# A recurrent spiking block with a top-2 mixture: expert 0 and the bias rows move from VectorE's sums to ScalarE reads and accumulating DMAs

## What is computed

```python
# attention-like part
R, K, V = x @ Wr.T, x @ Wk.T, x @ Wv.T          # then spikes by lif_scan
h = 0.9 * h + k * v;  y = r * h                  # over the 512 steps
x1 = layernorm(x + y @ Wo.T, g1, b1)
ffn = lif_scan(lif_scan(x1 @ W1.T + b1) @ W2.T + b2)
x2 = layernorm(x1 + ffn, g2, b2)
x3 = _layernorm(x + x2)
# mixture of 8 experts, the 2 best per token
gates = top-2 of softmax(x3 @ Wg + bg), normalised
moe = sum over e of gate[e] * (x3 @ We[e] + be[e])
out = _layernorm(x3 + moe)
```

## Time and profile before

| | |
|---|---|
| median of 3 runs | 1124.46 us (1119.31 to 1125.79) |
| the profiled execution, its own time | 1122.8 us |
| its span, first to last instruction | 1120.9 us |
| busy: PE / PE weight load / DVE / ACT / POOL | 86% / 83% / 91% / 49% / 64% |
| mean granted TensorE clock | 0.946 of 2.4 GHz |
| accumulating DMAs on POOL's queue | 192 of 256 KB |

### The profile page before, as it was taken

How to read it: one execution, slowest core, us unless ns; L and a number is a source line. 1 busy time by engine, 2 the same in 40 slices (tenths; PEclk the granted TensorE clock), 3 DMA queues, 4 the chain that set the end, 5 groups by cost and what they waited for, 6 DMA issues and landing times.

```text
span 1120.9 us, 21932 instructions
## 1 busy us (share of the span) xinstructions
PE 958.6 (86%) x7552; PEld 926.4 (83%) x7552; DVE 1024.0 (91%) x3257; ACT 545.4 (49%) x1270; POOL 715.7 (64%) x838
## 2 busy tenths in 40 slices
PE   3567679999999999999999999999999999889783
PEld 3456668888888998888888899888888998789783
DVE  6888998999999999999999999999999999998863
ACT  4223334455455555455455555445455555346353
POOL 5154432778777667777777776677777677774453
PEclk9768888999999999999999999999999999899997
DMA  6110002334343444434343444433333444335565
GB/s 200 33 48 29 29 29 48 66 77 94 81 87 74 90 86 89 89 69 95 81 87 75 90 95 85 85 86 77 78 80 79 95 86 82 71 75 105 105 114 112
DMA packets 49361, 91.31 MB, mean 81 GB/s; under 512 B 5473, under 2 KB 5473, under 8 KB 49249
## 3 DMA queue, kind: packets, MB, share of 16 engines
q0 software_dynamic: 27648, 50.34, 26.5%
q1 hardware_dynamic: 16992, 31.16, 8.8%
q10 hardware_dynamic: 4608, 8.39, 2.0%
HBM read 31.16 MB, written 8.39 MB: 35 GB/s over the span
## 4 chain that ended last, share of the span: by engine, by line
DVE 48%; PE 37%; issue 6%; POOL 4%; ACT 3%; DMA 2%; DVEq 0%; POOLq 0%; ACTq 0%
DVE U L710 11%; PE ps_e L342 10%; DVE V L717 9%; PE ps_proj L412 6%; PE ps_proj L397 6%; PE ps_proj L342 6%; PE ps_attn L378 4%; DVE stats L775 4%; DVE h L762 3%; DVE h L751 3%; PE ps_proj L418 3%; DVE y L768 2%; POOL x_lo L1127 2%; DVE x_lo L823 2%; DVE y L747 1%
## 5 line engine op out<-in xcount | busy, mean ns | idle before, releaser
L342 PE MATMUL ps_e<-we_hi,x_hi 128*128 128x256 f32 (+1 forms) x1024 | 293.4, 287 | 6.3 <-ACT odd_sum L583 6.3
L710 DVE SCALAR_TENSOR_TENSOR U<-V,U 128x256 f32<-128x256 f32 (+5 forms) x656 | 275.4, 430 | 15.2 <-ACT U L546 7.6
L342 PE MATMUL ps_e<-we_lo,x_hi 128*128 128x256 f32 (+1 forms) x1024 | 287.1, 280 | 0.0
L342 PE MATMUL ps_e<-we_hi,x_lo 128*128 128x256 f32 (+1 forms) x1024 | 287.0, 280 | 0.0
L717 DVE SCALAR_TENSOR_TENSOR V<-U 128x256 f32<-128x256 f32 (+5 forms) x656 | 259.9, 406 | 1.0
L546 ACT ACTIVATE U<-ps_proj,cst 128x256 f32<-128x256 f32 x320 | 135.7, 482 | 195.7 <-PE ps_proj L418 101.8
L1084 POOL TENSOR_SCALAR s<-U 128x256 fp32r<-128x256 f32 x208 | 223.2, 1099 | 1.1 <-DVE V L717 1.1
L342 PEld LDWEIGHTS ps_e<-we_hi,x_hi 128*128 128x128 f32 x1024 | 193.5, 189 | 7.3 <-ACT odd_sum L583 7.3
L342 PEld LDWEIGHTS ps_e<-we_hi,x_lo 128*128 128x128 f32 x1024 | 194.8, 190 | 0.1
L342 PEld LDWEIGHTS ps_e<-we_lo,x_hi 128*128 128x128 f32 x1024 | 193.5, 189 | 0.0
L583 ACT ACTIVATE term<-ps_e,gate 128x256 f32<-128x256 f32 x384 | 161.8, 476 | 51.1 <-PE ps_e L342 49.5
(11 more groups left out here) (89 smaller groups left out, 2396.0 us busy)
## 6 DMA issues: line engine op xcount, KB each, us to landing
acc<-term POOLq DMA_DIRECT2D x96, 256.0 KB, 3.5
odd_sum<-term POOLq DMA_DIRECT2D x96, 256.0 KB, 3.4
xt<-x_T SPq DMA_DIRECT2D x33, 256.0 KB, 3.0
xa<-x_tok SPq DMA_DIRECT2D x32, 256.0 KB, 4.3
xb<-x_tok SPq DMA_DIRECT2D x32, 256.0 KB, 2.7
out<-res ACTq DMA_DIRECT2D x32, 256.0 KB, 2.1
term<-w SPq DMA_DIRECT2D x8, 256.0 KB, 5.3
term<-w_e SPq DMA_DIRECT2D x7, 256.0 KB, 2.9
```

The costliest lines, as they stand in the source:

```text
L342: mm = pe.matmul(dst, lhs, rhs, start=(i == 0), stop=(i == n - 1))
L710: v.scalar_tensor_tensor(out=U[:, s, t, c0:c1], in0=V[:, c0:c1], scalar=0.5, in1=U[:, s, t, c0:c1], op0=ALU.mult, op1=ALU.add).then_inc(do ...
```

## The change

Expert 0's product is read by ScalarE (`read_expert0`, two instructions, scaled by the gate) into a seventh slot of `term`, ahead of expert 1 and between the two halves of `read_x1`. The bias product is copied by ScalarE into the eighth slot (`read_bias`, one instruction after expert 7). GpSimd issues two more accumulating DMAs per chunk. The even sum now lies on `x3` itself, which gets three copies; expert 0 is its first term. The bias is the last term of the odd sum. VectorE loses `add_e0` (two instructions) and `fin_stage` step 0 (one). GpSimd's order is new: the DMAs of 4 and 5, two parts of the spikes, those of 6 and 7, the other two parts, that of the bias, and then `add_bias`, the reciprocals and the rest.

```diff
+            def read_expert0(b):
+                act.wait_ge(e0_done, b.value(1, LAG_M, 1))
+                act.wait_ge(gate_steps, b.value(GATE_STEPS, LAG_M, GATES_DONE))
+                if some(b.value(ADDED, LAG_M + 1, 16)):
+                    act.wait_ge(even_added, b.value(ADDED, LAG_M + 1, 16))
+                for j in range(TILES):
+                    last = nc.scalar.activation(term_of(0)[:, j * D:(j + 1) * D], ps_e0[:, j, 0:D],
+                                                ACT.Identity, scale=gate[:, b.slot(LAG_M, 2), j, 0:1])
+                last.then_inc(e0_read, 1)
+            def read_bias(b):
+                act.wait_ge(bias_done, b.value(1, LAG_M, 1))
+                if some(b.value(ADDED, LAG_M + 1, ADDED)):
+                    act.wait_ge(odd_added, b.value(ADDED, LAG_M + 1, ADDED))
+                copy(term_of(E), ps_zx[:].rearrange("p j d -> p (j d)")).then_inc(bias_read, 1)
...
                     if k == 1 and b.has(LAG_M):
+                        read_expert0(b)
                         read_expert(b, 1)
...
                     for e in (5, 6, 7):
                         read_expert(b, e)
+                    read_bias(b)
...
-                v.scalar_tensor_tensor(out=acc[:, b.slot(LAG_M, 2), j, :], in0=ps_e0[:, j, 0:D],
-                                       scalar=gate[:, b.slot(LAG_M, 2), j, 0:1], in1=x3[:, j, :],
-                                       op0=ALU.mult, op1=ALU.add).then_inc(e0_added, 1)
...
-                    v.tensor_tensor(last_term, last_term, ps_zx[:], ALU.add).then_inc(fin_steps, 1)
...
-                    v.tensor_tensor(res[:], acc[:, b.slot(LAG_F, 2)], odd_sum[:, b.slot(LAG_F, 2)],
+                    v.tensor_tensor(res[:], x3[:, b.slot(LAG_F, 3)], odd_sum[:, b.slot(LAG_F, 2)],
...
-                    for part in range((FK - b.dve_spikes) // 2):
-                        spikes_h1(b, part)
+                parts = range((FK - b.dve_spikes) // 2) if b.has(LAG_S) else range(0)
                 if has_f:
                     add_even(b, LAG_F, 4)
                     add_odd(b, LAG_F, 5)
+                for part in parts[:2]:
+                    spikes_h1(b, part)
+                if has_f:
+                    add_even(b, LAG_F, 6)
+                    add_odd(b, LAG_F, 7)
+                for part in parts[2:]:
+                    spikes_h1(b, part)
+                if has_f:
+                    add_odd(b, LAG_F, E + 1)
                 if has_z:
                     add_bias(b)
...
                 if has_m:
+                    add_even(b, LAG_M, 0)
+                if has_f:
+                    reciprocal_std(b, 3, fin_steps, FIN_STEPS, LAG_F, 5)
+                if has_m:
                     add_even(b, LAG_M, 2)
-                if has_f:
-                    reciprocal_std(b, 3, fin_steps, FIN_STEPS, LAG_F, 6)
-                if has_m:
                     add_odd(b, LAG_M, 3)
```

More of the change, by code:

```diff
@@ L76 @@
 RAW_SLOTS = 4
-TERM_SLOTS = E - 2
+TERM_SLOTS = E
 ROW_HH, ROW_LH, ROW_HL = 0, 32, 64
 STACK = ROW_HL + E
-STEADY = dict(y=(0, 1, 2, 3, 4), z_sum=5, spikes_h1=7, fin_sum=5,
-              gate=(6, 7, 8, 9, 12, 13, 14, 14, 15, 16, 18, 20), add_e0=(18, 22),
+STEADY = dict(y=(0, 1, 2, 3, 4), z_sum=5, spikes_h1=7,
+              gate=(6, 7, 8, 9, 12, 13, 14, 14, 15, 16, 18, 20),
               ln1_sum=7, ln1_stats=(8, 9), ln1_aggr=10, ln1_norm=13,
@@ L92 @@
               fin_add=24, fin_stats=25, fin_aggr=26, fin_shift=28)
-FILL = dict(z_sum=-1, y=(-1,) * 5, spikes_h1=-1, fin_sum=-1,
-            gate=(4, 5, 6, 7, 9, 10, 10, 11, 12, 13, 17, 18), add_e0=(14, 15),
+FILL = dict(z_sum=-1, y=(-1,) * 5, spikes_h1=-1,
+            gate=(4, 5, 6, 7, 9, 10, 10, 11, 12, 13, 17, 18),
             ln1_sum=2, ln1_stats=(3, 4), ln1_aggr=5, ln1_norm=9,
@@ L98 @@
             fin_add=24, fin_stats=25, fin_aggr=26, fin_shift=31)
-DRAIN = dict(z_sum=-1, y=(-1,) * 5, spikes_h1=-1, fin_sum=-1,
-             gate=(-1, 0, 1, 2, 3, 4, 5, 6, 6, 7, 12, 13), add_e0=(11, 12),
+DRAIN = dict(z_sum=-1, y=(-1,) * 5, spikes_h1=-1,
+             gate=(-1, 0, 1, 2, 3, 4, 5, 6, 6, 7, 12, 13),
              ln1_sum=-1, ln1_stats=(-1, -1), ln1_aggr=-1, ln1_norm=4,
@@ L428, in expert0 @@
                 pe.wait_ge(x3_lo_ready, b.value(1, LAG_M, 1))
-                if some(b.value(2, LAG_M)):
-                    pe.wait_ge(e0_added, b.value(2, LAG_M))
+                if some(b.value(1, LAG_M)):
+                    pe.wait_ge(e0_read, b.value(1, LAG_M))
                 for j in range(TILES):
@@ L575, in read_expert @@
                 else:
-                    dst = term[:, e - 2, 0:PIECE]
-                    if some(b.value(ADDED, LAG_M + 1, 16 * (e // 2))):
-                        act.wait_ge(odd_added if e % 2 else even_added, b.value(ADDED, LAG_M + 1, 16 * (e // 2)))
-                if e == 1:
-                    act.wait_ge(gate_steps, b.value(GATE_STEPS, LAG_M, GATES_DONE))
+                    dst = term_of(e)
+                    place = 16 * (e // 2) if e % 2 else 16 * (e // 2 + 1)
+                    if some(b.value(ADDED, LAG_M + 1, place)):
+                        act.wait_ge(odd_added if e % 2 else even_added, b.value(ADDED, LAG_M + 1, place))
                 bank = (b.slot(LAG_M, 2) * (E - 1) + e - 1) % 2
@@ L602, in norm_x3 @@
                 act.wait_ge(ln3_steps, b.value(LN3_STEPS, LAG_Z, LN3_STEPS))
-                if b.has(LAG_M):
-                    act.wait_ge(e0_added, b.value(2, LAG_M, 2))
-                if some(b.value(1, LAG_Z)):
-                    act.wait_ge(x3T_done, b.value(1, LAG_Z))
-                normalised(2, x3, w).then_inc(x3_ready, 1)
+                if some(b.value(FIN_STEPS, LAG_Z + 3, 1)):
+                    act.wait_ge(fin_steps, b.value(FIN_STEPS, LAG_Z + 3, 1))
+                normalised(2, x3[:, b.slot(LAG_Z, 3)], w).then_inc(x3_ready, 1)
             def beat(b):
@@ L937, in side @@
                     spikes_h1(b)
-                if b.has(LAG_F) and slot == at["fin_sum"]:
-                    fin_stage(b, 0)
                 if b.has(LAG_Z):
@@ L981, in side @@
                         bn_aggr(b, 2, ln3_steps, LN3_STEPS, LAG_Z, 2)
-                if b.has(LAG_M):
-                    for j in range(TILES):
-                        if slot == at["add_e0"][j]:
-                            add_e0(b, j)
                 if b.has(LAG_Z) and slot == at["ln3_shift"]:
@@ L1094, in add_even @@
             def add_even(b, lag, e):
-                pool.wait_ge(term_ready, b.value(E - 1, lag, e))
-                if e == 2:
-                    pool.wait_ge(e0_added, b.value(2, lag, 2))
-                if some(b.value(ADDED, lag, 16 * (e // 2 - 1))):
-                    pool.wait_ge(even_added, b.value(ADDED, lag, 16 * (e // 2 - 1)))
-                g.dma_start(acc[:, b.slot(lag, 2)].rearrange("p j d -> p (j d)"), term[:, e - 2, 0:PIECE],
+                if e == 0:
+                    pool.wait_ge(e0_read, b.value(1, lag, 1))
+                else:
+                    pool.wait_ge(term_ready, b.value(E - 1, lag, e))
+                if some(b.value(ADDED, lag, 16 * (e // 2))):
+                    pool.wait_ge(even_added, b.value(ADDED, lag, 16 * (e // 2)))
+                g.dma_start(x3[:, b.slot(lag, 3)].rearrange("p j d -> p (j d)"), term_of(e),
                             accum_op=ALU.add).then_inc(even_added, 16)
             def add_odd(b, lag, e):
-                pool.wait_ge(term_ready, b.value(E - 1, lag, e))
+                if e > E:
+                    pool.wait_ge(bias_read, b.value(1, lag, 1))
+                else:
+                    pool.wait_ge(term_ready, b.value(E - 1, lag, e))
                 if some(b.value(ADDED, lag, 16 * (e // 2 - 1))):
                     pool.wait_ge(odd_added, b.value(ADDED, lag, 16 * (e // 2 - 1)))
-                if e == E - 1:
-                    pool.wait_ge(fin_steps, b.value(FIN_STEPS, lag, 1))
-                g.dma_start(odd_sum[:, b.slot(lag, 2)].rearrange("p j d -> p (j d)"), term[:, e - 2, 0:PIECE],
+                g.dma_start(odd_sum[:, b.slot(lag, 2)].rearrange("p j d -> p (j d)"), term_of(min(e, E)),
                             accum_op=ALU.add).then_inc(odd_added, 16)
```

33 lines of the change are left out of this document (10 added, 23 removed).

## The result

| | before | after |
|---|---|---|
| median | 1121.88 us (4 runs) | 1230.31 us (4 runs, 1227.96 to 1238.71) |
| profiled execution, its span | 1122.8, 1120.9 | 1231.67, 1229.8 |
| mean granted clock over the span | 0.946 | 0.923 |
| first to last start of `y` in 25 steady beats (mean) | 788.1 (31.5) | 856.7 (34.3) |
| last start of `y` to the end | 135.3 | 172.3 |

The ratio is 1.0988, with an interval of 1.0907 to 1.1069: slower, as forecast, but by 108 us where 28 were forecast. Of the 108.9 us between the two spans 68.6 lie in the steady beats (856.7 - 788.1), 37.0 behind them and 3.3 ahead of them.

The account below looks back on a forecast made before the run. It took a loop through TensorE (20.7 of a 31.0 us beat) as the bound, with VectorE on it only for `y`; 1122.8 + 15.6 + 3.9 + 9 = 1151.3, forecast 1151, eight in ten within 1132 to 1172.

Parts of the forecast that it names:

- What is removed is worth nothing: VectorE's three instructions, 1.62 us a beat, lie beside TensorE's unbroken 20.7 us; gain costed at nothing.
- Expert 0 ahead of expert 1, +15.6: ScalarE's extra read delays expert 1's read, holding TensorE up before expert 3: 0.6 us a beat, 26 beats.
- GpSimd's order, +3.9: New queue leaves the first reciprocal no slack; 0.15 us a beat for this and DMA issues beside `y` together.
- GpSimd becomes the bound: Rival, 13%: DMAs of 4 and 5 each wait 1 us, first reciprocal 2 us late; 1176 us.
- A longer beat gives the landings more time: Argument against the GpSimd rival: the waits for DMA landings shrink by themselves.
- DMA issues beside `y`: Two pairs of issues beside VectorE's `y`: bounds 0 and 0.4 us per pair; shares the +3.9 with the reciprocal.
- Drain and end, +9: Last beats: reciprocals behind all five DMAs, and one more odd-sum link of 3.4 us; bounds 3.4 and 15.
- Clock, 0: Number of slow-clock stretches, about nine, left as it is; bounds -12 and +8 us.
- VectorE's idle time grows before the first normalise: Sign of being right: idle time before `x3_low` or the first normalise grows by about 50 us.
- a new wait before expert 3: Sign of being right: TensorE waits for ScalarE's read of expert 1, about 0.6 us, 26 times.
- reciprocals of the drain behind accumulating DMAs: Sign of being right: in the drain the reciprocals start later, behind accumulating DMAs.
- not 50: Sign of being right: VectorE's busy time falls by about 50 us.

Follow-up runs that it names:

- e7: Kernel before, with VectorE's three instructions cut to 8 columns from the third chunk on and nothing put in their place: 1124.61 us, ratio 1.0006.
- e3: Kernel after, with ScalarE reading expert 1 first and expert 0 behind x1: 1224.71 us, ratio 1.0896.
- e5: Kernel after, with the bias DMA behind the second reciprocal and ScalarE reading expert 0 behind expert 1 and x1: 1178.09 us, ratio 1.0487.
- e11: e5 with the DMAs of terms 6 and 7 moved behind all the spikes: 1177.8 us, ratio 1.0479.
- e13: e6 with ScalarE reading expert 1 first and expert 0 behind x1: 1140.28 us, ratio 1.0161.
- e17: Kernel after, spikes first, terms 7 and 6 together behind the first reciprocal, bias DMA between split_x1's halves, expert 1 read first: 1167.33 us, ratio 1.0403.
- e6: Only expert 0's half of the change: bias stays on VectorE, GpSimd's order of before with one added DMA: 1148.9 us, ratio 1.0222.
- e14: Kernel after, with GpSimd issuing term 7 ahead of term 6: 1209.02 us, ratio 1.0748.
- e1: Kernel after, with the bias DMA issued behind add_bias and the second reciprocal: 1179.93 us, ratio 1.0511.
- e15: Kernel after without the bias DMA, the bias rows left out of the sum: 1172.52 us, ratio 1.0448.

## Why the direction was right and the size wrong

- **What is removed is worth nothing.** Right: e7.
- **Expert 0 ahead of expert 1, +15.6.** The stop is there: 0.92 us idle in the beat shown, 24.8 us in all, 15.5 of it in the steady beats. But taking it out gave only 2 to 9 us (e3, e5, e11, e13, e17); that another wait of the same loop is due next is shown by e3's waits. The half of the change that it belongs to costs 17.4 us in the steady beats (e6: 805.5 - 788.1), near the 15.6, and that nearness is in part luck: TensorE's recorded wait there is 3.4 us, and the order of the reads explains 4.5 (e6 to e13). The rest of the 17.4 stays open.
- **GpSimd's order, +3.9: the step that failed.** It read "a landing takes 3.2 to 6.7, median 3.4", and let every DMA ahead of the reciprocals go at once. The median was that of all 96 issues; the second of a pair at that very place took 5.1 to 6.7 in every one of ten beats. In the forecast's queue term 7 goes at +5.9 and the bias DMA at +10.8: by 3.4 it waits for nothing, by the 5.4 and 0.5 of the rows it waits 1.0, and 1.03 was measured. With the late start and term 5's 0.56 us this made the normalise behind the reciprocal 2.15 us late, not 0.15 for the whole term. Measured by parts, in the steady beats: 17 us for the landing of 7 and its 0.5 us later issue (after to e14: 856.7 - 839.7), 21 for the rest of the bias DMA in front (e14 to e1: 839.7 - 818.5), and 13 between e1 and e6 (818.5 - 805.5): e1 has four issues ahead of the first reciprocal, e6 two; the two differ in the bias copy and the bias DMA as well, but without that DMA (e15) 11 of the 13 stay. Together 51, against 3.9.
- **A rival came nearest.** "GpSimd becomes the bound" put the end of the spikes at +12.8 and the reciprocal's end at +16.5; they came at +12.5 and +16.7. It had 13%. It was right in the engine and the size, by another wait: it let the DMAs of 4 and 5 wait 1 us each, and measured were 0.56 for 5 and then 1.03 for the bias DMA, a wait that it didn't have. Its price was mis-sized: 1.7 us a beat replaced the stop before expert 3 instead of adding to it. With its own 2.0 plus 0.6, 26 beats give 67.6, and the steady beats measured 68.6; the closeness is partly luck, as the measured beats also hold the longer last instruction of the gates, which it didn't have. "A longer beat gives the landings more time" did not hold: the bias DMA waited 1.03 in a beat of 34.20. My reading is that the whole queue moves with the beat, so the distance of two issues in it stays.
- **DMA issues beside `y`.** Zero or less. In the 25 steady beats `y` ended 5.7 to 7.4 us after its start, 6.0 in the median, against 6.38 before. This is the place where the trace and the Trainium skill ("SBUF — State Buffer", Who interferes with whom) were weighed, and for `y` the rule, no contention of descriptor generation with such an instruction, fits. For line 717 of the earlier trace rows it does not: before, that instruction took 0.45 to 0.81 us beside the pair of issues, over 0.5 in 24 of 25 steady beats, where 0.41 is usual. Whatever stretched it cost the loop nothing. Before, spikes ran beside all of `y`; now issues take a part of that time.
- **Drain and end, +9.** Measured +37.0. Three parts: 6.5 with expert 0 (e6), 9.6 between e6 and e15 (not taken apart further), 20.9 with the bias DMA in front (e15 to after). The working gave 4.3 to one of the four beats, 1.8 to another and 3.4 to the last link; the rows show the bias DMA waiting in all four (4.50 to 2.91 us), and a link is 3.8. Some 3.3 us more lie in the fill, which had no term.
- **Clock, 0.** Right in its price: 0.98 and 0.97 in the steady stretch. The count of steady beats with a mean granted clock under 1.00 rose from 9 to 14, but they cost nothing any more. Before, they took 31.5 to 32.7 us against 30.9 to 31.1 (one, the first, 32.7); after, the 14 take 34.26 in the mean and the 11 at 1.00 take 34.28. This, too, says that TensorE no longer makes the beat.
- **What should have shown it.** "VectorE's idle time grows before the first normalise", "a new wait before expert 3", and "reciprocals of the drain behind accumulating DMAs" are all there. VectorE's busy time fell by 30 us, not 50. Of the 20 us between, 8.5 are the gates' line 896, which took 13.8 us in the steady beats and 5.3 before; that the rest too is other instructions beside other neighbours is argued only.

The Trainium skill ("DMA: Bandwidth & Descriptors", Anatomy of one DMA) says that a wait on a semaphore is made by the issuing sequencer before dispatch, not by the DMA engines. The 1.03 us of GpSimd's idle time before the bias issue is that rule in a row. Its fit of 2.0 us plus bytes over 436 GB/s gives an estimate of 2.6 us for 256 KB; accumulating from SBUF to SBUF took 3.2 at least here, and the measurement decides.
